# Turning the quantised activations of a feed-forward by transposing DMAs in place of TensorE transposes and PSUM copies

## What is computed

```
x  = x * rsqrt(mean(x*x) + 1e-6) * rmsnorm_weight
q, s   = quant(x)            # s = max(max|x| / 127, 1e-8) per token, q = round(x / s)
gate   = (q @ Wgq.T) * s * wsg.T      # 512 -> 1376
up     = (q @ Wuq.T) * s * wsu.T
h      = silu(gate) * up
q2, s2 = quant(h)
out    = (q2 @ Wdq.T) * s2 * wsd.T    # 1376 -> 512
```

## Time and profile before

| | |
|---|---|
| median of 3 runs | 437.66 us (437.33 to 438.32) |
| span of the profiled execution | 434.5 us |
| PE busy | 391.3 us (90%) |
| PE weight loads | 312.5 us (72%) |
| DVE busy | 278.4 us (64%) |
| ACT busy | 166.8 us (38%) |
| POOL busy | 178.7 us (41%) |
| chain that ended last, by engine | PE 73%, DVE 12%, issue 6%, POOL 4%, ACT 2%, DMA 1% |

### The profile page before, as it was taken

The page is one execution under the profiler, slowest core; times in us unless marked ns, Lnnn a source line. Parts: engine busy times, 40 slices in busy tenths (PEclk is TensorE's granted clock), DMA queues, the critical chain, the costliest instruction groups (busy, mean ns, idle before and its releaser), DMA issues.

```text
span 434.5 us, 6209 instructions
## 1 busy us (share of the span) xinstructions
PE 391.3 (90%) x2081; PEld 312.5 (72%) x2086; DVE 278.4 (64%) x465; ACT 166.8 (38%) x286; POOL 178.7 (41%) x154
## 2 busy tenths in 40 slices
PE   2939999999999999999999999997959758899993
PEld 1728888888888989888888888896847544455542
DVE  4816764433343458555655545658796999999993
ACT  4403753333333326433333313332432236555652
POOL 3876777655211051111113000074562661747561
PEclk9988999999999999999999999999888997999998
DMA  8946445444322459455556410253513360000102
GB/s 294 325 114 219 134 139 161 151 165 125 119 98 97 152 188 369 173 171 172 190 170 217 151 66 0 85 188 130 149 71 98 106 217 0 2 24 34 42 24 74
DMA packets 21662, 58.68 MB, mean 135 GB/s; under 512 B 3665, under 2 KB 6277, under 8 KB 21513
## 3 DMA queue, kind: packets, MB, share of 16 engines
q1 hardware_dynamic: 16977, 47.26, 31.6%
q0 software_dynamic: 4224, 10.36, 7.8%
q10 hardware_dynamic: 440, 0.79, 0.5%
HBM read 56.28 MB, written 2.12 MB: 134 GB/s over the span
## 4 chain that ended last, share of the span: by engine, by line
PE 73%; DVE 12%; issue 6%; POOL 4%; ACT 2%; DMA 1%; SPq 0%; DVEq 0%; ACTq 0%; POOLq 0%
PE ps L1207 26%; PE ps L1250 14%; PE ps L1429 8%; PE ps L1213 7%; POOL agu L401 4%; PE ps L1243 4%; PE ps L1325 3%; PE ps L1466 3%; PE ps L1332 2%; PE ps L1198 2%; DVE x_hl L798 1%; PE ps L1260 1%; PE ps L1380 1%; DVE cw L1070 1%; DVE qs L1078 1%
## 5 line engine op out<-in xcount | busy, mean ns | idle before, releaser
L1207 PE MATMUL ps<-x_hl,wg_hl 128*128 128x512 f32 x528 | 127.5, 391 | 0.1
L1207 PEld LDWEIGHTS ps<-x_hl,wg_hl 128*128 128x128 f32 x528 | 97.6, 188 | 20.5 <-issue 1.1
L414 POOL DMA_INDIRECT b_raw<-b_gu_dram,idx_all x44 | 42.8, 972 | 93.4 <-DVE b_hl L798 84.0
L889 DVE TENSOR_TENSOR act_raw<-ps,sil 128x512 f32<-128x512 f32 x22 | 15.2, 691 | 100.2 <-issue 68.2
L1250 PE MATMUL ps<-act_hl,wd_hl 128*128 128x512 f32 x264 | 64.0, 391 | 0.0
L1250 PEld LDWEIGHTS ps<-act_hl,wd_hl 128*128 128x128 f32 x264 | 48.2, 188 | 9.1
L466 POOL TENSOR_TENSOR t_raw<-t_raw,inv_b 128x1376 f32<-128x1376 f32 x8 | 25.8, 3242 | 61.6 <-DMA inv_b<-scale_scratch 49.7
L1429 PE MATMUL ps<-wq,qt 128*128 128x459 bf16 (+1 forms) x192 | 41.2, 368 | 4.1 <-DVE cw L1070 4.1
L401 POOL DMA_INDIRECT agu<-a_gu_dram,idx_a x32 | 36.5, 1141 | 14.8 <-issue 9.5
L574 ACT ACTIVATE sil<-ps 128x512 f32<-128x512 f32 x22 | 13.1, 596 | 73.9 <-PE ps L1213 73.9
L1213 PEld LDWEIGHTS ps<-tg_hl,b_hl 128*128 128x128 f32 x264 | 37.3, 190 | 4.4 <-issue 1.2
(11 more groups left out here) (155 smaller groups left out, 604.5 us busy)
## 6 DMA issues: line engine op xcount, KB each, us to landing
wg_raw<-w_gu_dram SPq DMA_DIRECT2D x22, 512.0 KB, 4.8
nat<-w_nat_dram SPq DMA_DIRECT2D x11, 768.0 KB, 4.3
wd_raw<-w_d_dram SPq DMA_DIRECT2D x22, 256.0 KB, 2.6
t_raw<-wg_t_dram SPq DMA_DIRECT2D x4, 688.0 KB, 6.1
t_raw<-wu_t_dram SPq DMA_DIRECT2D x4, 688.0 KB, 5.4
t_raw<-wd_t_dram SPq DMA_DIRECT2D x5, 512.0 KB, 3.6
out_dram<-r_sb SPq DMA_DIRECT2D x7, 256.0 KB, 2.0
vu_raw<-w_vu_dram SPq DMA_DIRECT2D x3, 512.0 KB, 9.4
```

Of the source, the lines that this page charges most:

```text
L414: gp.indirect_dma_start(out=b_raw[:, slot, g, :], out_offset=None, in_=a["b_gu"], in_offset=bass.IndirectOffsetOnAxis(ap=idx_all[:, f, 2 * ...
L1207: mm(bank[:], wg_hl[:, slot, w, gu * H + k * P:gu * H + (k + 1) * P], x_hl[n][:, v, k, :], start=(k == 0 and (w, v) == THREE[0]), stop=False)
```

## The change

It takes the 32 + 88 TensorE transposes of q1 and q2 away with the copies from PSUM on ACT and DVE, and has SP issue transposing DMAs from SBUF to SBUF: one per tile for q1 (`turn_q1`), two per tile for q2 (`turn_q2`). q2 is widened from 1376 to 1408 columns, so that the last block is whole, and DVE sets the added columns to zero once. SP's stream becomes: weight loads 3 to 8, the loads of the weight scales (`ws_b`, `wsd_b`) that stood behind load 13, load 9, then loads 10 to 13 each followed by a turn of q1, the remaining turns of q1, and then `store(t)` and `turn_q2(t + 2)` by turns. Each turn has a semaphore on which PE waits before it uses the tile, and ACT before it writes q1 or q2 again. A turn of q2 waits for the down projection two tiles earlier (`o_ready`) to free its slot of q2t. PE's steps are gate and up of three chunks, then down.

```diff
+            def turn_q1(t):
+                sp.wait_ge(q1_made, t + 1)
+                sp.dma_start_transpose(qt[:, t, :, :], q1[:, t % 4, :]).then_inc(qt_in[t], 16)
+
+            def turn_q2(t, slot):
+                if not (isinstance(t, int) and t < 2):
+                    sp.wait_ge(o_ready, t - 1)
+                for part in range(2):
+                    sp.wait_ge(q2_made, 2 * t + part + 1)
+                    sp.dma_start_transpose(q2t[:, slot, Q2T_PARTS[part], :],
+                                           q2[:, slot, Q2_TURN[part]]).then_inc(q2t_in[slot][part], 16)
+
+            for c in range(3, 9):
+                next_t(c)
...
+            next_t(9)
+            for c in range(10, 14):
+                next_t(c)
+                turn_q1(c - 10)
+            for t in range(4, TILES):
+                turn_q1(t)
...
-            with sp.Fori(0, TILES // 2 - 1) as j:
-                store(2 * j, 0)
-                store(2 * j + 1, 1)
+            turn_q2(0, 0)
+            turn_q2(1, 1)
+            for t in range(TILES - 2):
+                store(t, t % 2)
+                turn_q2(t + 2, t % 2)
             store(TILES - 2, 0)
...
                 if t >= 4:
-                    act.wait_ge(qt_ready, t - 3)
+                    act.wait_ge(qt_in[t - 4], 16)
                 nc.scalar.activation(q1[:, t % 4, :], cw[:, t % 3, :], ACT.Copy, bias=-ROUND).then_inc(q1_made, 1)
...
             def l1_step(t, slot):
                 l1_silu(t, slot, 0)
-                q2t_copy(t - 2, slot, 0)
                 l1_silu(t, slot, 1)
-                q2t_copy(t - 2, slot, 1)
                 q2_round(t - 1, 1 - slot)
                 l1_silu(t, slot, 2)
...
             dve.wait_ge(wsb_in, 48)
+            V.memset(q2[:, :, F:FP], 0.0)
...
             def l1_gate_up(t, c):
+                if c == 0 and isinstance(t, int):
+                    pe.wait_ge(qt_in[t], 16)
...
                 for j in range(FT):
                     if j in (0, 6):
-                        pe.wait_ge(q2t_out, 2 * t + (1 if j == 0 else 2))
+                        pe.wait_ge(q2t_in[slot][j // 6], 8 * (t - slot) + 16)
...
             def l1_step(t, slot):
-                l1_gate_up(t, 0)
-                l1_gate_up(t, 1)
-                q2_transpose(t - 2, slot, 0)
-                l1_gate_up(t, 2)
-                q2_transpose(t - 2, slot, 1)
+                for c in range(3):
+                    l1_gate_up(t, c)
                 l1_down(t - 2, slot)
```

More of the change, by code:

```diff
@@ L185, in build @@
     h_rnd = sb("h_rnd", [P, F], fp32, at=X0 + 16 * F)
[L186 to L190, removed]
+    q2 = sb("q2", [P, 2, FP], bf16, at=X0 + 20 * F)
+    q2t_at = X0 + 20 * F + 4 * FP
+    q2t = sb("q2t", [P, 2, FT, P], bf16, at=q2t_at)
+    o_sb = sb("o_sb", [P, 2, H], fp32, at=q2t_at + 5632)
+    r_sb = sb("r_sb", [P, 2, H], fp32, at=q2t_at + 9728)
+    assert q2t_at % 32 == 0 and q2t_at + 9728 + 4096 <= W0
     s_at = {"sall": slice(0, 4), "alpha": slice(4, 5), "beta": slice(5, 6), "s_r": slice(6, 7),
@@ L253, in build @@
         ms_made, s_step = sem("ms_made"), sem("s_step")
-        last_q2t_out, last_made = sem("last_q2t_out"), sem("last_made")
+        last_made = sem("last_made")
+        qt_in = [sem(f"qt_in{t}") for t in range(TILES)]
+        q2t_in = [[sem(f"q2t_in{slot}{part}") for part in range(2)] for slot in range(2)]
         ident_b, warmed = sem("ident_b"), sem("warmed")
@@ L362, in _, with next_t @@
             sp.dma_start(rmsw[:], a["rmsw"]).then_inc(rmsw_in, 16)
-            for c in range(3, 14):
+            def next_t(c):
                 sp.wait_ge(t_quant, c - 2)
                 load_t(c)
+            def turn_q1(t):
[10 more added lines that the diff above has]
+                next_t(c)
                 if c == 5:
@@ L725, in q2_round @@
                 if not (isinstance(t, int) and t < 2):
-                    act.wait_ge(q2t_ready, 2 * t - 2)
+                    for part in range(2):
+                        act.wait_ge(q2t_in[slot][part], 8 * (t - slot))
                 for i, cols in enumerate(Q2_PARTS):
@@ L1389, in cond_lora @@
                 last.then_inc(cond_ready, 1)
[L1391 to L1399, removed]
             pe.wait_ge(x1_lo, 8)
@@ L1431, in l1_gate_up @@
                     last.then_inc((gq_ready, uq_ready)[gu], 1)
[L1433 to L1440, removed]
-                for i, j in enumerate(blocks):
-                    m = min(P, F - j * P)
-                    last = tr(psb[bank][0:m, i * P:(i + 1) * P], q2[:, slot, j * P:j * P + m], identb[:])
-                last.then_inc(q2t_ready, 1)
             def l1_down_halves(t, slot):
                 pe.wait_ge(o_made, t)
-                pe.wait_ge(q2t_out, 2 * t + 1)
                 for i in range(2):
                     for j in range(FT):
-                        if i == 0 and j == 6:
-                            pe.wait_ge(last_q2t_out, 1)
+                        if i == 0 and j in (0, 6):
+                            pe.wait_ge(q2t_in[slot][j // 6], 8 * (t - slot) + 16)
                         m = min(P, F - j * P)
@@ L1484, in _ @@
                 l1_gate_up(0, c)
-                qt_transpose(TILES - 4 + c)
-            qt_transpose(TILES - 1)
             for c in range(3):
                 l1_gate_up(1, c)
-            pe.wait_ge(qt_out, TILES)
             pe.wait_ge(t_quant, 14)
-            for c in range(3):
-                l1_gate_up(2, c)
-            q2_transpose(0, 0, 0)
-            q2_transpose(0, 0, 1)
-            l1_down(0, 0)
+            l1_step(2, 0)
             l1_step(3, 1)
+            for t in range(4, TILES):
+                pe.wait_ge(qt_in[t], 16)
             with pe.Fori(0, TILES // 2 - 2) as j:
@@ L1499, in _ @@
                     l1_step(2 * j + 4 + d, d)
-            for t in (TILES - 2, TILES - 1):
-                first = t == TILES - 2
-                q2_transpose(t, t % 2, 0, parts_read=2 * t if first else 2 * t - 1)
-                pe.wait_ge(g_made, 3 * TILES)
-                q2_transpose(t, t % 2, 1, bank=0, parts_read=0 if first else 2 * t)
-                if t < TILES - 1:
-                    l1_down(t, t % 2)
-                else:
-                    l1_down_halves(t, t % 2)
+            l1_down(TILES - 2, 0)
+            pe.wait_ge(g_made, 3 * TILES)
+            l1_down_halves(TILES - 1, 1)
 def kernel(**inputs):
```

26 lines of the change are left out of this document (6 added, 20 removed).

## The result

The changed kernel takes 438.83 us (median of 20 runs, 437.02 to 440.52) against 437.06 us of the kernel before in the same rounds: ratio 1.0037, 95% interval 1.0023 to 1.0052. That is 1.6 us slower (1.0 to 2.3), where 1.7 was forecast. The sign and the size were right. Two of the terms in the sum were not, and the largest one was taken on a path that the span does not wait for; that the total agrees is luck.

What follows compares the result with a forecast made beforehand. DVE was taken to bound the feed-forward at 7.33 us a tile. Gains of 1.45 + 0.43 less 0.4 at down(0) put DVE 1.5 us earlier; the later tail left net 1.7 us lost: 437.66 + 1.7 = 439.4 us, range 436.6 to 447.

Steps and rivals of the forecast that it cites:

- The bound, and the steady part: Feed-forward: DVE sets 7.33 us a tile; dropping q2's PE transposes gains only what PE cost DVE, 0.43 us in all.
- budget of 5.8 us: Steady q2 loop: a landing up to 5.8 us is free; beyond it half the excess is lost a tile.
- The start, 1.45 us: Feed-forward start: 0.7 us from PE being ahead, 0.7 from ACT freed of qt copies; together 1.45 us gained.
- the 0.7 from PE: Feed-forward start: with 1.10 us less PE work in front, tile 1's evacuations end at 372.05, not 372.76; 0.7 gained.
- worth nothing: Modulation stage: four of q1's eight transposes lie in PE's idle gaps, so removing them gains nothing.
- The landing, 4.0 us: q2's transposing DMA: part 0 lands 4.0 us after its making, issue included; part 1 follows 1.5 us later.
- rival A: Short landing of q2's DMAs, 2.0 to 3.3 us: 436.6 us at 2.4, 438.0 at 3.3; chance 0.30.
- The tail, 3.15 us of loss in the forecast: After the last tile: the down projection's halves wait for q2t's DMA landings, ending at 430.65 against 428.97.
- Before down(6) a fall is hidden: down(6): at the low clock it ends near 426.3, before the last q2t lands, so nothing is lost.
- PE's clock, kept for the range with one chance in three: Before down(0): PE's clock falling while it stands still would cost up to 1.9 us; chance one in three.
- +0.4 at down(0): Tile 0's down projection waits for q2's part 1 until 381.05 and ends at 382.15, not 381.75: 0.4 us lost.
- SP's queue and the modulation stage: Weight loads late by a turn's issue and moved broadcasts cost nothing, at worst 2 us; rival E +1 to +3, chance 0.04.

Runs made afterwards that it cites:

- one-turn: Changed kernel with one transposing DMA per tile of q2 (128x1408) in place of two; ratio 1.0059 (1.0030 to 1.0089) to the kernel before.

## Why the prediction was right, point by point

**The bound, and the steady part.** Right. DVE sets a tile's 7.33 us, and 0.62 us less of PE a tile brought only what PE had cost: 29.75 to between 29.30 and 29.32 in all kernels with q2 by DMA, 0.43 as forecast. PE's steady wait for q2t is nil, as its budget of 5.8 us said.

**The start, 1.45 us.** The mechanism was right, and with the clock up so was the size: q1 alone by DMA has 0.76 + 0.69. In the changed kernel's first profile the 0.7 from PE is missing, since PE stays at the low clock until 366.7: a term that I had not seen. Of the four transposes of q1 between the `cond` calls I had written that they lie in PE's idle gaps, "worth nothing". Without them PE's idle stretch ahead of the feed-forward grew from 4.06 us to 9.64, and in three of the nine profiles with that stretch the low clock reached further into the feed-forward, at a cost of some 0.9 us.

**The landing, 4.0 us.** Wrong: 2.7 from the part's making, 2.5 from issue. The estimate scaled the gather's 2.9 by bytes up to 4.35; one-turn shows that size hardly counts, and the plain store's 2.0 was the nearer row. Part 1 followed by 1.1 to 1.2 us, 1.5 had been taken. This was rival A's landing, and its formula gives -1.45 - 0.43 - 1.65 + 2.7 + 0.5 = -0.3: by the landing that was measured, the forecast's own sum would have said level, and the kernel is 1.6 us slower. The landing does not make that loss. With the extra matmuls before down(0) and down(6), and every turn still by DMA, the kernel is 1.1 us faster than the one before.

**The tail, 3.15 us of loss in the forecast** (4.0 - 1.65 + 0.8). This was the largest term, and it was taken on the wrong path. The tail did grow, by 1.7 us (7.44 against 5.72), but nothing waits for it: POOL's closing DRAIN ends 2.4 us after the rest before and 2.6 after. The chain that the earlier trace rows is taken from ends at 429.94 with the last busy instruction, and the span at 434.5; what fills those 4.6 us was not asked. The chain that counts goes through down(6), of which the prediction says "Before down(6) a fall is hidden". There the changed kernel loses 1.96 us in the first profile and 2.93 in the repeated one. With down(6) at the high clock the loss is 0.65 (9.68 against 9.03), which is what the later landing costs; the other 1.3 to 2.3 us are the low clock.

**PE's clock, kept for the range with one chance in three.** It should have been in the sum, at three places. A fall at down(0) costs 1.22 us (8.55 against 7.33), not 1.9, and was seen in four of seven profiles; at the start 0.9 us in three of nine; at down(6) in seven of seven, 1.3 to 2.4 us where a tile has two turns. The halves were at the low clock in two profiles, 1.4 and 1.7 us longer, for which the span did not wait. Set beside each other, the forecast has -1.45 at the start, -0.43 in the steady part, +0.4 at down(0) and +3.15 in the tail, together +1.7. The first profile has -0.61, -0.44, +1.22 and, at down(6), +1.96, together +2.1; the repeated one -1.56, -0.43, nothing and +2.93, together +0.9. The medians say +1.6 and +1.0. So the forecast's 1.7 is right by luck: a loss that costs nothing stands in for one that it had at nothing.

**SP's queue and the modulation stage.** Right: from the second to the sixth, cw multiplications are 4.72 to 4.79 us apart after and 4.76 to 4.78 before, and no load is late for POOL.

What stays open: how often the clock falls at each of the three places in an ordinary execution. Each kernel has one profile, but of each execution the mean granted clock is on record. Of the changed kernel's 20, the seven with 0.953 or 0.954 have a median of 439.3 us and the thirteen from 0.956 up one of 438.1. With one turn per tile the five up to 0.960 took 441.2 to 442.3 us and the seven from 0.963 up 437.5 to 439.5. So outside the profiles too the executions with the lower mean clock are the slower ones, but the mean does not tell the place. Also open is the first layer's length, which differs by up to 2.5 us between profiles though its code is the same; of the changed kernel's two profiles, the second is 2.2 us ahead as early as 42 us from the start. The first cw comes at 332.9 us on average in the ten profiles with q2 by DMA and at 332.1 in the four with q2 on PE; whether the change has a part in these 0.8 us, the scatter of 2.5 us does not let one say.

The version that beats both kernels is the one that turns only q1 by DMA: 435.34 us, ratio 0.9953 (0.9933 to 0.9973), since q1's turns are hidden and free ACT at the one place where it held up others, while q2's leave PE idle ahead of down(0) and down(6), where its low clock is then on the chain.

## What to carry to other kernels

Split such a change by where the result is awaited: a turn by DMA is free where several microseconds lie between making and use, as for q1 and for q2 in the steady part. At the pipeline's fill and drain PE waits for it, and the wait itself cost little here (nothing at down(0), 0.65 us at down(6)); dear was the low clock of the matmuls that follow the wait. Work taken off a PE that is not the bound brings only what PE cost the bound, and the gaps that it leaves are not free: put a low-clock rerun of what follows each lengthened gap into the sum. Find what the span really ends with: if it goes on for microseconds after the chain's last instruction, look for each engine's last instruction and see which of them keeps the same distance to the end in every profile. Before a difference between two profiles is explained, look at a point ahead of the change, and profile the same kernel twice.

## What the runs showed of the hardware

A transposing DMA from SBUF to SBUF holds SP for 1.19 to 1.38 us where a plain store takes 0.34, nearly independent of its size, and lands by the median 2.4 to 3.1 us after issue for 128 to 352 KB (3.7 at most).

The granted clock of TensorE after idle times of 2.05 to 3.4 us was at either level, twice at the same place in the same program (2.28 us low, 2.05 high). After 4.15 to 4.72 us it was low in all seven profiles. The fall can come when the matmuls have begun again: in the kernel with q1 on PE down(0) begins at 381.74, and the clock falls at 382.8. Ahead of the feed-forward, after the 9.64 us, it was low in both profiles of the changed kernel and rose during the matmuls that followed, in one at some 363.0 us and in the other at some 366.7.

GpSimd's closing DRAIN starts with its last instruction, takes 9.2 us in all 14 profiles and ends the span; what it does in that time no run shows.
